# Dilated attention: the head of an eight-batch pipeline rearranged, in one stage of a two-layer kernel

## The reference, cut to what matters

```python
x = x + tanh(g_xattn[1]) * attention(layernorm(x), ctx, ctx, ...)

def attention(query, key, value, Wq, bq, ..., Wo, bo):      # 16 heads of 16 numbers
    q, k, v = query @ Wq.T + bq, key @ Wk.T + bk, value @ Wv.T + bv
    for sl, dr in zip([256, 512, 1024], [1, 2, 4]):          # segment length, dilation
        scores = einsum(q, k) * D ** -0.5                    # causal, per segment
        lse = logsumexp(scores); o = einsum(exp(scores - lse), v)
    w = softmax over the three lse                           # mixes the three outputs
    return sum(o * w) @ Wo.T + bo
```

## Time and profile before

| | |
|---|---|
| median of three runs | 826.72 us (823.61 to 829.61) |
| the profiled execution | 827.62 us, its span 825.9 us |
| busy in the span | PE 653.9, DVE 497.5, ACT 432.9, POOL 354.7 us |
| granted TensorE clock, mean | 0.881 |
| block of the dilated attention | from 412.5 to about 688 us |
| turns -3, -2, -1 | up to 423.6, 444.1 and 464.5 us |

### The profile page before, as it was taken

One profiled execution on the slowest core, in us unless ns is written; L12 is line 12 of the kernel. 1 busy time (PEld: TensorE's weight loads), 2 busy tenths in 40 slices (PEclk: granted clock), 3 DMA queues, 4 the chain that ended last, 5 costly groups with the idle time before them and its releaser, 6 DMA issues. The chain is left out here.

```text
span 825.9 us, 14463 instructions
## 1 busy us (share of the span) xinstructions
PE 653.9 (79%) x4946; PEld 479.1 (58%) x4946; DVE 497.5 (60%) x1624; ACT 432.9 (52%) x829; POOL 354.7 (43%) x482
## 2 busy tenths in 40 slices
PE   2989999549999999999644687778787982179995
PEld 2777777328788777877512345555454551046774
DVE  0467665856666666664115567797776445867741
ACT  1354432227866876687121465567555636427652
POOL 2133335473563365354422442445344414534653
PEclk9999999859999999999875797799887897569998
DMA  6235214273563555342221121233120413503433
GB/s 198 79 112 166 69 53 154 90 207 111 107 161 99 108 136 153 93 91 33 33 70 33 50 81 45 71 90 105 53 61 10 128 52 121 181 27 71 90 54 38
DMA packets 73882, 76.08 MB, mean 92 GB/s; under 512 B 8037, under 2 KB 66449, under 8 KB 73553
## 3 DMA queue, kind: packets, MB, share of 16 engines
q1 hardware_dynamic: 61217, 59.32, 23.1%
q0 software_dynamic: 10928, 15.57, 11.3%
q10 hardware_dynamic: 1664, 0.27, 0.2%
HBM read 52.20 MB, written 22.94 MB: 91 GB/s over the span
## 5 line engine op out<-in xcount | busy, mean ns | idle before, releaser
L1977 DVE CUSTOM_DVE_ANT_0 c_sn<-c_ps_s,k_mask 128x128 f32<-128x128 f32 (+1 forms) x256 | 75.8, 352 | 57.3 <-PE c_ps_s L2115 57.2
L1756 POOL TENSOR_SCALAR_AFFINE_SELECT c_pr<-c_pr 128x512 f32<-128x512 f32 x64 | 43.3, 676 | 114.2 <-ACT c_pr L1855 113.2
L1398 PE MATMUL b_ps_y<-e_w2h,b_hh 128*128 128x256 f16 x320 | 87.4, 273 | 1.4 <-DVE b_yb L1312 0.6
L1398 PE MATMUL b_ps_y<-e_w2h,b_hl 128*128 128x256 f16 x320 | 87.3, 273 | 0.0
L1398 PE MATMUL b_ps_y<-e_w2l,b_hh 128*128 128x256 f16 x320 | 87.3, 273 | 0.0
L1281 DVE TENSOR_TENSOR b_hl<-b_h,b_hh 128x640 f16<-128x640 f32 x64 | 53.2, 832 | 47.5 <-ACT b_hh L1229 47.5
L1207 POOL DMA_INDIRECT res<-b_y,b_s_idx x40 | 65.3, 1631 | 37.7 <-ACT b_y L1246 27.4
L1193 POOL DMA_INDIRECT e_xg<-rows,e_g_idx x35 | 38.6, 1104 | 81.8 <-DVE e_g_idx L1322 71.2
L2143 PE MATMUL c_ps_v<-c_pr,k_vx 128*64 128x256 f32 (+1 forms) x512 | 64.3, 379 | 4.7 <-POOL c_pr L1756 4.0
L1855 ACT ACTIVATE c_pr<-c_ps_t 128x768 f32<-128x768 f32 x64 | 51.7, 808 | 15.8 <-PE c_ps_t L2129 15.8
L2115 PE MATMUL c_ps_s<-k_ks,c_qs 48*128 48x128 f16 (+1 forms) x256 | 24.9, 279 | 42.8 <-DVE c_mx L1977 27.5
(11 more groups left out here) (423 smaller groups left out, 1835.9 us busy)
## 6 DMA issues: line engine op xcount, KB each, us to landing
e_w<-in_L_ffn_W_dram SPq DMA_DIRECT2D x16, 1024.0 KB, 5.9
s_raw<-in_L_ffn_W_down_dram SPq DMA_DIRECT2D x8, 640.0 KB
k_ks<-kT SPq DMA_DIRECT2D x48, 64.0 KB, 2.8
c_qs<-q SPq DMA_DIRECT2D x48, 64.0 KB, 2.4
s_raw<-in_L_ffn_W_up_dram SPq DMA_DIRECT2D x4, 682.0 KB, 4.2
rows<-a_rows SPq DMA_DIRECT2D x8, 264.0 KB, 2.7
rows<-s_rows SPq DMA_DIRECT2D x8, 264.0 KB, 2.2
a_x_in<-in_x_dram SPq DMA_DIRECT2D x8, 256.0 KB, 3.3
```

The lines of the kernel that those rows point to most:

```text
L1398: last = pe.matmul(ps_y[(j + CT) % 2][:, 0:D], a, b[:, f, :], start=(f == 0 and k == 0), stop=(f == FC - 1 and k == 2))
L1756: pool.affine_select(out=late, in_=late, compare_op=ALU.is_ge, fill=0.0, base=0, pattern=[[0, 2], [0, 2], [1, P]], channel_multiplier=-1). ...
L1977: dve.tensor_tensor_reduce(sn[r][:, a:b], ps_s[:, r, a:b], mask[:, a:b], -1.0, 3.0e38, ALU.add, ALU.min, mx[g % 2][:, q, r, j:j + 1]).then ...
```

## The change

Three batches' rows are loaded before the first turn instead of one. The statistics of batch 1 move to slot 0 of turn -2 (DVE, behind the low queries of batch 0). Its transposes and query product move to slot 0 of turn -2 on PE, behind 22 new `keep_busy` matmuls and ahead of the first scores. Its low queries move from slot 0 of turn -1 to slot 6 of turn -2 on DVE, behind pair 2 of batch 0. The scores of batch 0 use `ps_s` and `ps_t` in turn, so that those of pair j+1 wait for the maxima of pair j-1. In turn -1 the turn of `mhl` of batch 0 stands ahead of the first scores of batch 1, and the first key scores and exponentials of batch 0 stand in slot 6 instead of slot 7. For every batch, the stores of high and low queries have semaphores of their own, and the four loads of the high part wait for the high store alone.

```diff
-        sn = some(2, "sn", [P, QK])
+        sn = some(4, "sn", [P, QK])
-        s_qst = [sem("qst0"), sem("qst1")]; s_mst = [sem("mst0"), sem("mst1")]
+        s_qsh = [sem("qsh0"), sem("qsh1")]; s_qsl = [sem("qsl0"), sem("qsl1")]
+        s_mst = [sem("mst0"), sem("mst1")]
+        def first_scores_in_t(g, j):
+            return g == 0 and j % 2 == 1
...
# SP
-            load_x(0)
+            for first in range(3):
+                load_x(first)
...
                     landed(sp, s_ldq, f, 2, 96)
                     apart(sp, s_passs)
-                    after(sp, s_qh, f)
-                    after(sp, s_ql, f)
-                    for part, src in enumerate((qh, ql)):
+                    for done_, stored, part, src in ((s_qh, s_qsh, 0, qh), (s_ql, s_qsl, 1, ql)):
+                        after(sp, done_, f)
                         sp.dma_start(dram["q"][f % 2, part]..., src[f % 2][:])\
-                            .then_inc(s_qst[f % 2], 16)
-                    landed(sp, s_qst, f, 0, 32)
+                            .then_inc(stored[f % 2], 16)
+                    landed(sp, s_qsh, f)
                     done(sp, s_pt, (f - 2) * HH)
                     for part, which in enumerate((0, 0, 1)):
+                        if part == 2:
+                            landed(sp, s_qsl, f)
                         for r in range(2):
...
-                if within(e + 1):
+                if within(e + 1) and e + 1 >= 3:
                     load_x(e + 1)
# ACT
-                    if p + 1 == HH and within(g):
+                    if p + (2 if g == 0 else 1) == HH and within(g):
                         exps(g, 0)
# DVE
             def maxima(g, j):
                 after(dve, s_ps, g * HH + j)
+                bank = ps_t if first_scores_in_t(g, j) else ps_s
...
+            def queries_low(f):
+                after(dve, s_qh, f)
+                landed(dve, s_qsl, f, 2)
+                dve.tensor_tensor(ql[f % 2][:], qf[:], qh[f % 2][:], ALU.subtract).then_inc(s_ql, 1)
...
-                    if p == 0 and within(f):
-                        ... (the same three lines)
+                    if p == 0 and within(f) and f != 1:
+                        queries_low(f)
+                    if p == 6 and e == 1:
+                        queries_low(e)
...
-                    if p == 4 and within(e):
+                    if p == (0 if e == 1 else 4) and within(e):
                         landed(dve, s_ldx, e)
                         after(dve, s_nmr, e, 2)
                         stats(e, ...)
# PE
             def scores(g, j):
-                done(pe, s_mx, (g * HH + j) * 4)
+                done(pe, s_mx, (j - 1 if g == 0 else g * HH + j) * 4)
+                bank = ps_t if first_scores_in_t(g, j) else ps_s
...
             def step(n):
                 for p in range(HH):
+                    if p == 0 and e == 1:
+                        keep_busy(22)
+                        rows_turn(e)
+                        queries(e)
                     if p + 1 < HH and within(n):
                         by_keys(n, p + 1)
-                    if p + 1 == HH and within(g):
+                    if p + (2 if g == 0 else 1) == HH and within(g):
                         by_keys(g, 0)
                     if p < 4 and within(g):
                         scores(g, p + 4)
+                    if p == 4 and g == 0:
+                        maxima_turn(n, g)
                     if p >= 4 and within(f):
                         scores(f, p - 4)
-                    if p == 4 and within(g):
-                        ... (the turn of mhl, written out)
+                    if p == 4 and within(g) and g > 0:
+                        maxima_turn(n, g)
...
-                    if p == 6 and within(e):
-                        ... (waits and turn(ps_a, xn[e % 2], swap=True))
-                    if p == 7 and within(e):
-                        ... (waits and product(ps_b, wT[:, 0], xT))
+                    if p == 6 and within(e) and e != 1:
+                        rows_turn(e)
+                    if p == 7 and within(e) and e != 1:
+                        queries(e)
```

More of the change, by code:

```diff
@@ L1735, in _ @@
             for u in range(2):
-                for pair, per in ((s_qst, 32), (s_mst, 16)):
+                for pair, per in ((s_qsh, 16), (s_qsl, 16), (s_mst, 16)):
                     sp.wait_ge(pair[u], per * B // 2)
@@ L1936, in step @@
                         after(act, s_qf, e)
-                        landed(act, s_qst, e, 2, 32)
+                        landed(act, s_qsh, e, 2)
                         act.activation(qh[e % 2][:], qf[:], ACT.Copy).then_inc(s_qh, 1)
@@ L1976, in maxima @@
                     for q, (a, b) in enumerate(((0, P), (P, QK))):
-                        dve.tensor_tensor_reduce(sn[r][:, a:b], ps_s[:, r, a:b], mask[:, a:b], -1.0, 3.0e38,
+                        dve.tensor_tensor_reduce(sn[2 * (j % 2) + r][:, a:b], bank[:, r, a:b], mask[:, a:b], -1.0, 3.0e38,
                                                  ALU.add, ALU.min, mx[g % 2][:, q, r, j:j + 1]).then_inc(s_mx, 1)
+            def queries_low(f):
+                after(dve, s_qh, f)
+                landed(dve, s_qsl, f, 2)
+                dve.tensor_tensor(ql[f % 2][:], qf[:], qh[f % 2][:], ALU.subtract).then_inc(s_ql, 1)
             def step(n):
@@ L2002, in step @@
                         maxima(f, p - 4)
-                    if p == 0 and within(f):
-                        after(dve, s_qh, f)
-                        landed(dve, s_qst, f, 2, 32)
-                        dve.tensor_tensor(ql[f % 2][:], qf[:], qh[f % 2][:], ALU.subtract).then_inc(s_ql, 1)
+                    if p == 0 and within(f) and f != 1:
+                        queries_low(f)
+                    if p == 6 and e == 1:
+                        queries_low(e)
                     if p == 4 and within(l):
@@ L2114, in scores @@
                         a = 64 * r
-                        last = pe.matmul(ps_s[:, r, lo:hi], q[a:a + 3 * HD, j, rows_], key[a:a + 3 * HD, j, 0:keys],
+                        last = pe.matmul(bank[:, r, lo:hi], q[a:a + 3 * HD, j, rows_], key[a:a + 3 * HD, j, 0:keys],
                                          start=True, stop=True)
@@ L2156, in turned, with maxima_turn, rows_turn, queries @@
                 last.then_inc(s_ot, 1)
+            def maxima_turn(n, g):
+                after(pe, s_mlo, g)
+                done(pe, s_av, n * HH + 4)
+                for q in range(2):
+                    last = pe.matmul(ps_v[0:4 * HH, T + (1 - q) * P:T + (2 - q) * P],
+                                     mhl[g % 2][:, q, :, :, :].rearrange("p r l b -> p (r l b)"), ident_h[:],
+                                     start=True, stop=True)
+                last.then_inc(s_pm, 1)
+            def rows_turn(e):
+                after(pe, s_xn, e, 0, 2)
+                after(pe, s_oT, e, 4)
+                if e:
+                    after(pe, s_xT, e - 1)
+                turn(ps_a, xn[e % 2], swap=True).then_inc(s_pxt, 1)
+            def queries(e):
+                after(pe, s_xT, e)
+                after(pe, s_x3, e, 4, 2)
+                if e:
+                    after(pe, s_qf, e - 1)
+                product(ps_b, wT[:, 0], xT).then_inc(s_pq, 1)
             def probabilities_turn(l, queries_out):
@@ L2186, in step @@
                         scores(g, p + 4)
+                    if p == 4 and g == 0:
+                        maxima_turn(n, g)
                     if p >= 4 and within(f):
                         scores(f, p - 4)
-                    if p == 4 and within(g):
-                        after(pe, s_mlo, g)
-                        done(pe, s_av, n * HH + p)
-                        for q in range(2):
-                            last = pe.matmul(ps_v[0:4 * HH, T + (1 - q) * P:T + (2 - q) * P],
-                                             mhl[g % 2][:, q, :, :, :].rearrange("p r l b -> p (r l b)"), ident_h[:],
-                                             start=True, stop=True)
-                        last.then_inc(s_pm, 1)
+                    if p == 4 and within(g) and g > 0:
+                        maxima_turn(n, g)
                     if within(n):
@@ L2243, in step @@
                             keep_busy(18)
-                    if p == 6 and within(e):
-                        after(pe, s_xn, e, 0, 2)
-                        after(pe, s_oT, e, 4)
-                        turn(ps_a, xn[e % 2], swap=True).then_inc(s_pxt, 1)
-                    if p == 7 and within(e):
-                        after(pe, s_xT, e)
-                        after(pe, s_x3, e, 4, 2)
-                        product(ps_b, wT[:, 0], xT).then_inc(s_pq, 1)
+                    if p == 6 and within(e) and e != 1:
+                        rows_turn(e)
+                    if p == 7 and within(e) and e != 1:
+                        queries(e)
             for n in range(-3, B + 2):
```

## The result

The changed kernel takes **814.19 us** (median of four runs, 809.86 to 819.01), the kernel before, beside it, 828.16 us (823.61 to 830.77): ratio 0.9847, 95% interval 0.9807 to 0.9887. By this ratio the change takes 12.7 us off, between 9.4 and 16.0, where 10.4 were predicted. The medians themselves lie 14.0 apart; the runs of either kernel spread over 7 to 9 us.

What follows compares the result with a forecast made beforehand. Turns -2 and -1 were taken as chains of waits, chiefly PE waiting for queries from memory. 9.0 + 1.4 = 10.4 us off 827.62 gives 817.2; the median lies 0.90 lower: 816.3 us, range 812.5 to 821.

Steps and rivals of the forecast that it cites:

- Second product ahead, first scores: Turn -2: product of batch 1 ends at 433.2, idle matmuls cost 0, first scores at 433.25, 0.45 us later.
- Two banks, low queries: Turn -2 on DVE: eight pairs at 1.12 us plus 0.69 for low queries, `mhl` at 443.85 against 451.57.
- Queries of batch 1: Turn -1: queries back at 443.4, PE wants them at 444.3, so the 3.38 us wait goes.
- Turn of `mhl` first: Turn -1 on PE: turn of `mhl` starts at 443.9, scores of batch 1 follow 0.4 later at 444.3.
- The marker: Key scores of pair 1 in turn 0: 455.5 instead of 464.51, 9.0 us earlier.
- Key scores in slot 6: Turn -1: maxima rows back between 448.5 and 450.2, costing 0 to 1.2 us; taken as 0.
- Stores apart, later batches: Turn 0: loads start at 468.2 instead of 469.64, 1.4 us off the 2.56 us wait; full turns 0.
- Three loads: Row loads before the first turn: one more added load costs between 0 and 2.4 us; taken as 0.
- Sum: Whole kernel: 9.0 + 1.4 = 10.4 us off the profiled execution's 827.62, giving 817.2.
- the clock holds better in turn 0: Rival, turn 0: the shorter wait may save the half clock that follows, worth 2.2 us: 815.2; chance 0.12.
- The second product at 1.2 GHz: Rival, turn -2: transposes and product of batch 1 at the lower clock, 2.2 us more: 818.5, or 820.6; chance 0.20.
- The forecast of 818.5 "by that rule": Turn -2: by the skill's rule that waits between bursts bring back the lower clock, 818.5 would be the forecast.

Runs made afterwards that it cites:

- third product ahead: Changed kernel with statistics, transposes and product of batch 2 also moved to turn -2, the product between the scores of batch 0: 812.95 us, ratio 0.980 to 0.987.
- two banks alone: Kernel before with only the scores of batch 0 in two pairs of banks in turn: one run, key scores of pair 1 in turn 0 at 40.22 us.

## Why the prediction was right, step by step

The time (816.3 predicted, 814.19 measured) and the mechanism held, with one term mis-sized and some luck in the clock. Against the first high queries as zero:

- *Second product ahead, first scores.* Predicted 8.8 us, measured 8.55. The idle matmuls end 1.4 us before the transposes and cost nothing.
- *Two banks, low queries.* `mhl` predicted done at 19.4, measured 18.95, at 1.11 us a pair.
- *Queries of batch 1.* The wait of 3.38 us is gone. How near it was: with the stores joined it is 0.54.
- *Turn of `mhl` first.* The scores of batch 1 came at 19.3 (19.8 predicted), but the order itself gains nothing and at an equal clock costs 0.7 us, as its own run shows.
- *The marker.* 9.0 us earlier predicted, 10.2 and 8.9 against the two profiles before. From the scores of batch 1 to the marker I took the old 11.24 us; it is 10.53, because the product of batch 2 takes 3.0 us instead of 3.7. The clock does that from profile to profile, so these 0.7 us are luck.
- *Key scores in slot 6.* At 23.1, 0.9 us ahead of my lower bound (24.0): 0.4 because `mrow` started earlier, and 0.5 because the way from there to the key scores took 3.7 us instead of 4.2. The transposes of batch 2 wait for ACT, not for them: 0, as taken.
- *Stores apart, later batches.* This term was mis-sized: 1.4 us predicted; turn 0 is shorter by 2.6 than in the first profile and by 1.9 than in the second, and with the stores joined again it is 3.2 longer. The loads leave 1.7 us earlier behind the marker than in the first profile (1.4 than in the second). What I had wrong is the time from loads to scores: I kept the 5.41 us of one profile (475.05 - 469.64), in which the transfer was slow. The second profile of the kernel before has 4.62, with a wait of 1.49 us at its end, and the changed kernel 4.55 and 4.73. So nearly the whole wait goes, and not 1.4 us of it. Over the kernels of the table turn 0 takes 19.2 to 19.3 us wherever PE waits at most 0.25 us for these queries and the clock is up within about 1 us of A, and 0.6 to 3.2 us more where it waits 1.0 to 2.6 us with the clock up as early; a longer wait is not always the dearer one.

```profile
472.12 2.72 SPq L1707 DMA_DIRECT2D c_qs<-q  x6
476.74 0.34 PE L2115 MATMUL c_ps_s<-k_ks,c_qs 48*128 48x128 f16 x4 [1.49 <-DMA c_qs<-q]
```

- *Three loads.* DVE's wait for the first rows is 1.5 us where it was 1.62: 0, as taken.
- *Sum.* 10.4 predicted; 12.8 and 10.8 at B against the two profiles before, with 12.7 (9.4 to 16.0) in the whole time. Nothing behind B gives it back: B to the end is 197.9, and 199.3 or 202.3 before.

Of the rivals, *the clock holds better in turn 0* did come true, as an addition: 1.00 instead of 0.90. But in the first profile it was not the source of the time. From A to the first scores of batch 2 it is 8.02 us instead of 10.54, the wait; from there to B 11.24 instead of 11.34, at full clock and at 0.85. With the stores joined it is the larger part: 13.07 us from those scores to B, at 0.61. *The second product at 1.2 GHz* did not happen in the changed kernel. Without the idle matmuls it happened just as priced (2.2 us, 3.8 for the product and 0.45 more in the transposes). With them it happened once in the nine profiles that have them: in the run with the third product ahead the product of batch 1 took 3.60 us. The Trainium skill ("TensorE: Matmul & The Clock Gate", HAM oscillation) says that a long wait between bursts of matmuls brings the lower clock back. The run without idle matmuls agrees (idle 6.18 us, then the product at the lower level). The forecast of 818.5 "by that rule" was not the page's: its waits are of several us, the gap in question 1.1. In the changed kernel 1.45 us of idle time left the product at full speed, and 1.44 us did not in the run with 3.60, so idle time alone does not settle it here.

The first two profiles alone would have misled. They lie 17.8 us apart: 10.2 up to A, 2.6 in turn 0, 5.9 behind B (4.4 in the block and 1.5 behind it), less 0.9 by which the first high queries came later.

## What to carry to other kernels

In the filling of a pipeline, write down for each engine what the next step waits for, and move forward the work that another batch's transfer hangs on; a faster step in front of a transfer that isn't there yet (two banks alone) only lengthens the wait. Before a product is moved to an idle place, look at what it did for the clock where it stood: where this one stood right ahead of turn 0, that turn had full clock from about its first us on; hiding it gave 2.5 us, and the half clock that followed took up to 1.5 back. Compare stages by marks inside the block, ask of each difference which product ran at which clock, and profile the same kernel twice; a stretch that no edit touched differed by 3.7 us between two profiles of one kernel. Two runs with equal marks can hide two effects that cancel, as the order of the `mhl` turn did.

## What the runs showed of the chip that I had not expected

The last turn of the block has two lengths, 49.1 to 49.4 and 52.8 to 53.2 us, for the same instructions: the granted clock falls to 0.78 or 0.88 in one stretch, or not at all, and which it is changes from one profile to the next of one kernel. A wait of PE in a busy turn can cost more than itself: 1.47 us idle, then half clock, 3.2 us in all (stores joined); but in the kernel before 2.56 us of the same wait left the next scores at full speed (0.34 us) and cost 2.6. What decides between the two was not settled. The same idle matmuls, an idle time of 0.6 to 1.45 us and a product gave 1.99 us for the product in eight profiles; in a ninth, with 1.44 us idle, it took 3.60. And 22 matmuls on data that nobody reads bought 2.2 us.
